# Bulk loads moved to GpSimd's queue, inputs and output laid out by partition, 19 tables packed into two transfers, first keys issued by ScalarE

## Chip, cores and metric

The kernel runs on one core of a Trainium2 chip. The metric is the device time of one execution in microseconds (us), as the median of several runs.

## What is computed

The reference is a two-layer transformer over x of shape 8 x 256 x 128, with a context of the same size and a mask of 8 x 1 x 256 x 256. Each of six sublayers is followed by a residual add and a layernorm:

```
x = LN(x + L0 self attention(x))            # 16 heads of 8, rotary angles on q and k
x = LN(x + L0 cross attention(x, ctx, ctx)) # causal, with a linear bias per head
x = LN(x + L0 ffn(x))                       # 64 of every 512 rows are picked by a router, attention + SwiGLU on them
x = LN(x + L1 self attention(x))            # with a Gaussian bias per query and head
x = LN(x + L1 cross attention(ctx, ctx, x, mask))
x = LN(x + L1 ffn(x))                       # mixture of 8 experts, top 2
```

## The kernel before, in words

Tokens lie on the 128 partitions in 16 tiles (X, f32, P x 16 x 128); XT is the same transposed. Five engines have an instruction list each, written out by hand, and are held together by semaphores.

**The first line.** The two first attention cores (`core_a0`: 8 items, `core_x0`: 8 items; one item is one batch of 256 tokens) run as one software pipeline, class `Line`, in steps; an item has 8 steps, one per pair of heads. At step s TensorE computes for item s // 8 the row maxima's scores (L616, read by VectorE's reduction L787) and, ten steps later (`LAG`), the scores again, transposed (L623 or L633), which ScalarE exponentiates (L745); TensorE then multiplies with the values (L682). The negated maxima go in as extra contraction rows: GpSimd casts them in two bf16 parts (L851, L852), TensorE turns them (L665), ScalarE copies them out (MT, L754), and SyncE (SP) writes them by DMA into the query operand (`m_rows`, L900, shown as `BIG<-MT`, two DMAs for each half item). TensorE may not start the scores of that half item before these have landed (`m_in`).

**How q and k get in.** `Split` makes three bf16 parts of each f32 projection: for each of 4 chunks of 512 tokens there are two jobs, q and k. One job is: two projections (TensorE L328), two multiplications with cos and sin (VectorE L360), their sum (GpSimd `add_turns`, L371, fbuf), first part (ScalarE L383), rest (`first_rest`, GpSimd L389, rbuf), second part (ScalarE L423), third part (GpSimd L428). SP writes the parts to DRAM (`write`, L436, rows_q and rows_k) and loads them again as operands for each item (`load`, L882: 6 DMAs for q, 6 for k, and L885: 2 of extra rows for q in the first items). Chunk 0 is done ahead of step 0, in a prologue; the others are worked in by each engine's `side(step)`.

**SP's queue.** SP works through its list in order; its `side(step)` also issues the bulk loads of what comes later: half the mask at step 6 (`Mask.load`, L1529, 1 MB), the transposed context at 13 (1 MB), the other 15 weights at 14 (0.96 MB), x at 21 (1 MB in rows of 512 bytes), the other half of the mask at 23, the context at 37, and 19 tables by one DMA each at 40, 42 and 44. TensorE, ScalarE and VectorE wait for the tables at step 63; the first use of the weights and of x is at step 39, of the transposed context at step 24 (GpSimd), of the context in `core_x0`'s values. After the last sublayer SP stores X in four DMAs (`out`, L1858).

Of the kernel before, what the change touches and what calls it, by code (L numbers as in the profile page):

```python
# [100 lines left out]
class Split:  # L101
# [283 lines left out]
    def first_rest(self, pool, n):  # L385

        pool.wait_ge(*self.s1_ready.at(n + 1))
        after(pool, self.s3_ready, n - 1)
        self.g.nc.gpsimd.tensor_tensor(self.g.rbuf[n % 2][:, :], self.source(n), self.part(n, 0), ALU.subtract)\  # L389
            .then_inc(self.r1_ready.sem, 1)  # L390
# [1123 lines left out]
class Mask:  # L1514
# [11 lines left out]
    def load(self, sp, half):  # L1526
        if half == 1:
            sp.wait_ge(*self.made.at(4))
        sp.dma_start(self.stage(half).rearrange("p (n k) -> p n k", k=S),  # L1529
                     self.g.io["mask"].rearrange("(n p) k -> p n k", p=P)[:, 8 * half:8 * half + 8, :])\  # L1530
          .then_inc(self.loaded.sem, 16)
# [107 lines left out]
class Experts:  # L1639
# [191 lines left out]
    def sync(self, sp, out):  # L1831
# [24 lines left out]
        for c in range(NC):  # L1856
            sp.wait_ge(*self.normed.at(c + 1))
            sp.dma_start(out.rearrange("(t p) d -> p t d", p=P)[:, c * TC:(c + 1) * TC, :],  # L1858
                         g.X[:, c * TC:(c + 1) * TC, :]).then_inc(self.stored.sem, 16)
# [157 lines left out]

class Globals:
# [20 lines left out]
    def allocate(self):  # L2039
# [41 lines left out]
        self.cols = sb("cols", [P, len(COLUMNS)])  # L2081
        self.rowvecs = sb("rowvecs", [P, len(ROWVECS), D])
        self.causal_q = sb("causal_q", [P, 2 * S], BF16)
        self.causal_k = sb("causal_k", [P, 2 * S], BF16)
# [6 lines left out]
        self.depth_q = sb("depth_q", [P, P], BF16)  # L2091
        self.depth_k = sb("depth_k", [P, P], BF16)
        self.router = sb("router", [P, P])
        self.earlier = sb("earlier", [P, 2, S])
        self.iota = sb("iota", [P, P])
        self.f0_w12 = sb("f0_w12", [P, 2, F0])
        self.f0_w3 = sb("f0_w3", [P, 3, D])
        self.upz = sb("upz", [P, 2 * H])
        self.router_w = sb("router_w", [P, EX])
        self.router_b = sb("router_b", [P, EX])  # L2100
        self.descending = sb("descending", [P, EX])
        self.multiples = sb("multiples", [P, T // P])
        self.up_to = sb("up_to", [P, EX, EX])
        self.upper_bf = sb("upper_bf", [P, P], BF16)
        self.ones_bf = sb("ones_bf", [P, P], BF16)
# [12 lines left out]
def program(nc, io, out):  # L2118
    with ExitStack() as ctx:
# [86 lines left out]
        def _(sp):  # L2206
# [13 lines left out]
            line.first_loads(sp, core_a0.items)  # L2220

            def side(step):
# [516 lines left out]
```

## Time and profile before

| | |
|---|---|
| median of 3 runs | 976.7 us (976.18 to 982.54) |
| profiled execution, its own time | 972.38 us |
| its span, first to last instruction | 970.5 us |
| mean granted TensorE clock | 0.871 |
| busy TensorE / VectorE / ScalarE / GpSimd | 79% / 62% / 51% / 24% of the span |
| GpSimd's DMA queue (q0), SP's (q1) | 7.21 MB, 67.18 MB |

The span is measured inside the execution, the own time around it. The busy shares are means over stages of different kinds; the first line takes the span's first 305 us or so. A "granted clock" of 1.00 is TensorE's upper level, 2.4 GHz, and 0.50 its lower, 1.2 GHz.

### The profile page before, as it was taken

Reading aid. Unit: us, or ns where it says so; the run is one execution under the profiler, and the core shown is the slowest. Engines: PE = TensorE matmul, PEld = TensorE weight load, DVE = VectorE, ACT = ScalarE, POOL = GpSimd, SP = SyncE. Lnnn points to the kernel's source line nnn. Section 1 sums busy time; section 2 is a strip of 40 time slices with the busy share of each in tenths; the row PEclk is TensorE's granted clock in tenths of the full one; section 3 lists DMA queues with packets and bytes.
Section 4 is the critical chain, followed back from the end, with each engine's and each line's share of the span. In section 5 each row is a group of like instructions: output and inputs, shape, how many; then the busy total and the mean of one; then the engine's idle time right before and its main releaser. Section 6 shows DMA issues by size and latency. Waiting matters only on the chain.

```text
span 970.5 us, 20640 instructions
## 1 busy us (share of the span) xinstructions
PE 763.2 (79%) x7108; PEld 416.7 (43%) x7109; DVE 604.1 (62%) x1908; ACT 498.5 (51%) x847; POOL 232.1 (24%) x390
## 2 busy tenths in 40 slices
PE   2687888999996645866749999999999529999950
PEld 1232323454443332434412333333334429999950
DVE  1476878667665823336348988877885344555576
ACT  1146767656556321512706877666656326665620
POOL 3344522223010120100501132323100062404223
PEclk8588999999998865956957999999999759999985
DMA  5466452242201123000532222221200611212212
GB/s 118 105 194 204 121 157 77 73 125 58 69 24 62 33 65 76 13 1 1 154 91 72 72 58 77 83 62 51 68 20 2 260 50 47 78 50 70 64 49 62
DMA packets 76075, 75.57 MB, mean 78 GB/s; under 512 B 21377, under 2 KB 65153, under 8 KB 75217
## 3 DMA queue, kind: packets, MB, share of 16 engines
q1 hardware_dynamic: 73504, 67.18, 24.1%
q0 software_dynamic: 2480, 7.21, 2.3%
q8 instruction: 54, 0.88, 0.4%
q14 instruction: 37, 0.30, 0.1%
HBM read 50.66 MB, written 23.13 MB: 76 GB/s over the span
## 4 chain that ended last, share of the span: by engine, by line
PE 61%; DVE 16%; ACT 5%; POOL 5%; issue 5%; DMA 4%; SPq 3%; POOLq 0%; DVEq 0%; ACTq 0%
PE PS L616 12%; PE PS L682 12%; PE PS L1874 8%; PE PS L633 8%; DVE MS L787 5%; PE PS L696 4%; PE PS L1884 4%; PE PS L328 2%; PE PS L623 2%; ACT X L1113 2%; POOL experts_x L1785 2%; PE PS L1047 1%; SPq L882 1%; DVE CX L804 1%; DMA OT<-experts_x 1%
## 5 line engine op out<-in xcount | busy, mean ns | idle before, releaser
L787 DVE TENSOR_REDUCE MS<-PS 128x2 f32<-128x512 f32 (+2 forms) x448 | 250.3, 592 | 130.3 <-PE PS L633 63.1
L745 ACT ACTIVATE BIG<-PS 128x1024 f32<-128x1024 f32 (+2 forms) x288 | 259.8, 906 | 63.2 <-PE PS L623 38.2
L616 PE MATMUL PS<-BIG 62*128 62x256 bf16 (+1 forms) x1088 | 199.3, 277 | 73.5 <-DMA BIG<-rows_k 16.5
L623 PE MATMUL PS<-BIG 64*128 64x256 bf16 (+1 forms) x1088 | 183.9, 269 | 1.2 <-DMA BIG<-MT 1.2
L682 PE MATMUL PS<-BIG,VA 128*32 128x256 f32 (+1 forms) x2176 | 166.7, 379 | 3.4 <-ACT OT L738 3.2
L616 PEld LDWEIGHTS PS<-BIG 62*128 62x128 bf16 x1088 | 68.5, 95 | 206.1 <-issue 97.2
L738 ACT COPY OT<-PS 128x256 f32<-128x256 f32 (+1 forms) x144 | 51.8, 360 | 117.3 <-PE PS L682 117.2
L1874 PE MATMUL PS<-OT,VA 128*128 128x128 f32 x736 | 96.7, 279 | 0.4 <-ACT OT L1931 0.4
L1874 PEld LDWEIGHTS PS<-OT,VA 128*128 128x128 f32 x736 | 91.4, 196 | 0.6 <-ACT OT L1931 0.6
L851 POOL CAST MB<-MS 128x16 bf16<-128x16 f32 (+1 forms) x72 | 14.2, 198 | 294.7 <-DVE MS L787 158.2
L682 PEld LDWEIGHTS PS<-BIG,VA 128*32 128x32 f32 x2176 | 43.4, 109 | 74.5 <-issue 63.7
L1926 ACT COPY VA<-BIG 128x1024 f32 x46 | 48.1, 1046 | 43.2 <-PE PS L1874 40.7
L623 PEld LDWEIGHTS PS<-BIG 64*128 64x128 bf16 x1088 | 64.0, 95 | 8.7 <-issue 4.0
L1965 DVE SCALAR_TENSOR_TENSOR turn<-fbuf,PS 128x512 f32<-128x512 f32 x46 | 31.6, 688 | 55.1 <-ACT fbuf L1941 55.1
L696 PE MATMUL PS<-ident,OT 128*128 128x128 f32 x272 | 59.6, 305 | 4.0 <-DVE CX L804 3.4
L782 DVE CUSTOM_DVE_ANT_0 Y<-PS,mask_q 128x256 f32<-128x256 f32 x128 | 48.8, 419 | 20.2 <-PE PS L616 19.6
L1884 PE MATMUL PS<-BIG,rbuf 128*128 x368 | 49.2, 277 | 0.9 <-DVE Y L1979 0.9
L782 DVE CUSTOM_DVE_ANT_0 HN<-PS,mask_q 128x256 f32<-128x256 f32 x128 | 48.9, 420 | 0.0
L1785 POOL DMA_INDIRECT experts_x<-X,experts_row x32 | 30.9, 965 | 72.8 <-DVE experts_row L1764 42.3
L696 PEld LDWEIGHTS PS<-ident,OT 128*128 128x128 f32 x272 | 28.0, 143 | 44.5 <-issue 41.5
L302 POOL TENSOR_TENSOR parts<-rbuf,parts 128x512 bf16<-128x512 f32 x14 | 17.1, 1224 | 124.7 <-ACT parts L227 124.6
L1884 PEld LDWEIGHTS PS<-BIG,rbuf 128*128 128x128 f32 x368 | 44.7, 192 | 1.4 <-issue 1.2
(238 smaller groups left out, 1062.6 us busy)
## 6 DMA issues: line engine op xcount, KB each, us to landing
rows_q<-parts SPq DMA_DIRECT2D x32, 192.0 KB, 2.1
rows_k<-parts SPq DMA_DIRECT2D x32, 192.0 KB, 2.1
BIG<-rows_q SPq DMA_DIRECT2D x64, 96.0 KB
BIG<-rows_k SPq DMA_DIRECT2D x64, 96.0 KB
BIG<-in_ex_w SPq DMA_DIRECT2D x3, 2048.0 KB, 12.1
BIG<-rows_q SPq DMA_DIRECT2D x64, 64.0 KB
BIG<-rows_k SPq DMA_DIRECT2D x64, 64.0 KB
OT<-experts_x SPq DMA_DIRECT2D x46, 64.0 KB, 1.8
```

The costliest lines, as they stand in the source:

```text
L616: return nc.tensor.matmul(bank[:, first:first + kw], g.Q6[b.buf][rows, u, qt * P:(qt + 1) * P], g.K6[b.buf][rows, u, 0:kw], start=start, s ...
L623: return nc.tensor.matmul(g.bank[2 * (v % 2) + a][:, core.offset[kt]:core.offset[kt] + n], g.K6[b.buf][rows, v, kt * P:(kt + 1) * P], g.Q6 ...
L633: return nc.tensor.matmul(core.biased(bank), g.ident_bf[:, :], bias, start=False, stop=True)
L682: last = nc.tensor.matmul(g.bank[6][PVW * hh:PVW * hh + PVW, lo:lo + w], g.VA[b.par][:, kt, 8 * (hh % 2) + 2 * grp + hh // 2, :], g.PT[grp ...
L696: last = nc.tensor.transpose(g.bank[7][:, grp * P:(grp + 1) * P], g.OT[b.par][:, grp, qt * P:(qt + 1) * P], g.ident[:, :])
L738: nc.scalar.copy(g.OT[b.par][:, grp, 0:w], g.bank[6][:, 0:w]).then_inc(self.ot_done.sem, 1)
L745: nc.scalar.activation(g.PT[v // 2 % 2][:, 2 * (v % 2):2 * (v % 2) + 2, 0:w], g.bank2[v % 2][:, :, 0:w], ACT.Exp, scale=SCALE).then_inc(se ...
L782: last = nc.vector.tensor_tensor_reduce(b.core.sums[a][:, 2 * qt:2 * qt + 2, :].rearrange("p n d -> p (n d)"), self.ring_bank["mx", step, ...
L787: nc.vector.tensor_reduce(g.MS[:, 0:n, a, u], self.ring_bank["mx", step, a][:, 0:n * w] .rearrange("p (n k) -> p n k", n=n), axis=AX_X, op ...
L1785: nc.gpsimd.indirect_dma_start(self.xs, bass.IndirectOffsetOnAxis(ap=self.row[:, k, n:n + 1], axis=0), g.X[:, n, :], None).then_inc(self.s ...
L1874: last = nc.tensor.matmul(g.bank[2 * a + b.par][:, f * P:(f + 1) * P], self.wb[b.par][:, a, f * P:(f + 1) * P], self.xt[b.par], start=True ...
L1884: last = nc.tensor.matmul(g.bank[6][:, 0:D], self.hid[b.par][:, f * P:(f + 1) * P], self.w3[:, bass.ds(e, 1), f, :].rearrange("p e d -> p ...
```

## The change

- The six bulk loads of the first line (both halves of the mask, transposed context, weights, x, context) are issued by GpSimd in its own `side(step)`, at the same step numbers, behind GpSimd's other work of that step.
- The mask, x and the context are stored in DRAM by partition, so that one partition's part of a transfer is one run of 8 KB; the output likewise, 2 KB in each of the four stores. The transposition is in the host's layout code.
- The 19 tables are packed into one f32 tensor (1.2 MB) and one bf16 tensor (0.39 MB), and GpSimd loads them at steps 28 and 32; the waits for them count 2 transfers in place of 19.
- In the prologue `first_rest` of the first two jobs is done by VectorE (behind its four multiplications), later ones stay on GpSimd; and the k operand of the first item is loaded from ScalarE's DMA queue, behind ScalarE's part of the prologue. SP loads that item's q and both operands of the second item.

```diff
@@ -382,11 +382,11 @@
         act.wait_ge(*self.rotated.at(n + 1))
         self.g.nc.scalar.copy(self.part(n, 0), self.source(n)).then_inc(self.s1_ready.sem, 1)
 
-    def first_rest(self, pool, n):
-
-        pool.wait_ge(*self.s1_ready.at(n + 1))
-        after(pool, self.s3_ready, n - 1)
-        self.g.nc.gpsimd.tensor_tensor(self.g.rbuf[n % 2][:, :], self.source(n), self.part(n, 0), ALU.subtract)\
+    def first_rest(self, eng, nc_eng, n):
+
+        eng.wait_ge(*self.s1_ready.at(n + 1))
+        after(eng, self.s3_ready, n - 1)
+        nc_eng.tensor_tensor(self.g.rbuf[n % 2][:, :], self.source(n), self.part(n, 0), ALU.subtract)\
             .then_inc(self.r1_ready.sem, 1)
 
     def take(self, act, n):
@@ -1526,9 +1526,7 @@
     def load(self, sp, half):
         if half == 1:
             sp.wait_ge(*self.made.at(4))
-        sp.dma_start(self.stage(half).rearrange("p (n k) -> p n k", k=S),
-                     self.g.io["mask"].rearrange("(n p) k -> p n k", p=P)[:, 8 * half:8 * half + 8, :])\
-          .then_inc(self.loaded.sem, 16)
+        sp.dma_start(self.stage(half), self.g.io["mask"][:, 8 * half * S:(8 * half + 8) * S]).then_inc(self.loaded.sem, 16)
 
     def make(self, dve, n):
 
@@ -1855,8 +1853,7 @@
         self.steps(sp, step, second_half)
         for c in range(NC):
             sp.wait_ge(*self.normed.at(c + 1))
-            sp.dma_start(out.rearrange("(t p) d -> p t d", p=P)[:, c * TC:(c + 1) * TC, :],
-                         g.X[:, c * TC:(c + 1) * TC, :]).then_inc(self.stored.sem, 16)
+            sp.dma_start(out[:, c * TC:(c + 1) * TC, :], g.X[:, c * TC:(c + 1) * TC, :]).then_inc(self.stored.sem, 16)
         sp.wait_ge(*self.stored.at(16 * NC))
...
@@ -2013,6 +2010,20 @@
            "x1_q", "x1_k", "x1_v", "x1_o", "f0_q", "f0_k", "f0_v", "f0_o"]
 COLUMNS = ["a1_bq", "a1_bk", "a1_bfq", "a1_bfg", "f0_g1", "f0_g2"]
 ROWVECS = ["a1_bv", "a1_bo", "x1_bo"]
+
+
+TABLES = {
+    F32: [("cols", (len(COLUMNS),)), ("router", (P,)), ("iota", (P,)), ("upz", (2 * H,)), ("router_w", (EX,)),
+          ("router_b", (EX,)), ("descending", (EX,)), ("multiples", (T // P,)), ("rowvecs", (len(ROWVECS), D)),
+          ("up_to", (EX, EX)), ("earlier", (2, S)), ("f0_w12", (2, F0)), ("f0_w3", (3, D))],
+    BF16: [("causal_q", (2 * S,)), ("causal_k", (2 * S,)), ("depth_q", (P,)), ("depth_k", (P,)),
+           ("upper_bf", (P,)), ("ones_bf", (P,))],
+}
+
+
+def tables_width(dt):
+
+    return sum(int(np.prod(shape)) for _, shape in TABLES[dt])
 
 
...
-        self.f0_w3 = sb("f0_w3", [P, 3, D])
-        self.upz = sb("upz", [P, 2 * H])
-        self.router_w = sb("router_w", [P, EX])
-        self.router_b = sb("router_b", [P, EX])
-        self.descending = sb("descending", [P, EX])
-        self.multiples = sb("multiples", [P, T // P])
-        self.up_to = sb("up_to", [P, EX, EX])
-        self.upper_bf = sb("upper_bf", [P, P], BF16)
-        self.ones_bf = sb("ones_bf", [P, P], BF16)
+        self.tables = {dt: sb(f"tables_{n}", [P, tables_width(dt)], dt) for n, dt in enumerate(TABLES)}
+        place = {}
+        for dt, entries in TABLES.items():
+            first = 0
+            for name, shape in entries:
+                w = int(np.prod(shape))
+                ap = self.tables[dt][:, first:first + w]
+                place[name] = ap if len(shape) == 1 else ap.rearrange("p (a b) -> p a b", a=shape[0])
+                first += w
+        self.cols, self.router, self.iota, self.upz = (place[n] for n in ("cols", "router", "iota", "upz"))
+        self.router_w, self.router_b = place["router_w"], place["router_b"]
+        self.descending, self.multiples = place["descending"], place["multiples"]
+        self.rowvecs, self.up_to, self.earlier = place["rowvecs"], place["up_to"], place["earlier"]
+        self.f0_w12, self.f0_w3 = place["f0_w12"], place["f0_w3"]
+        self.causal_q, self.causal_k = place["causal_q"], place["causal_k"]
+        self.depth_q, self.depth_k = place["depth_q"], place["depth_k"]
+        self.upper_bf, self.ones_bf = place["upper_bf"], place["ones_bf"]
 
...
@@ -2217,7 +2226,8 @@
             sp.dma_start(g.ident[:, :], io["ident"]).then_inc(ident_in.sem, 16)
             for n in range(2):
                 split_a0.write(sp, n)
-            line.first_loads(sp, core_a0.items)
+            line.load(sp, core_a0.items[0], "q")
+            line.load(sp, core_a0.items[1])
 
...
                             split_a0.write(sp, 2 * c + i)
-                if step == 6:
-                    mask.load(sp, 0)
-                if step == 13:
-                    sp.dma_start(g.CTXT[:, :], io["ctxt"]).then_inc(ctxt_in.sem, 16)
-                if step == 14:
-                    sp.dma_start(g.W[:, n_a0:, :], io["weights"][:, n_a0:, :]).then_inc(weights_in.sem, 16)
-                if step == 21:
-                    sp.dma_start(g.X[:, :, :], io["x"].rearrange("(t p) d -> p t d", p=P)).then_inc(x_in.sem, 16)
-                if step == 23:
-                    mask.load(sp, 1)
-                if step == 37:
-                    sp.wait_ge(*mask.made.at(8))
-                    sp.dma_start(g.CTX[:, :, :], io["ctx"].rearrange("(t p) d -> p t d", p=P)).then_inc(ctx_in.sem, 16)
-                if step == 40:
-                    for ap, name in ((g.cols, "cols"), (g.causal_q, "causal_q"), (g.causal_k, "causal_k"),
-                                     (g.depth_q, "depth_q"), (g.depth_k, "depth_k"), (g.router, "router"), (g.iota, "iota")):
-                        sp.dma_start(ap[:, :], io[name]).then_inc(tables_in.sem, 16)
-                if step == 42:
-                    for ap, name in ((g.upz, "upz"), (g.router_w, "router_w"), (g.router_b, "router_b"),
-                                     (g.descending, "descending"), (g.multiples, "multiples"), (g.upper_bf, "upper_bf"),
-                                     (g.ones_bf, "ones_bf")):
-                        sp.dma_start(ap[:, :], io[name]).then_inc(tables_in.sem, 16)
-                if step == 44:
-                    for ap, name in ((g.rowvecs, "rowvecs"), (g.up_to, "up_to"), (g.earlier, "earlier"), (g.f0_w12, "f0_w12"),
-                                     (g.f0_w3, "f0_w3")):
...
-                    pe.wait_ge(*tables_in.at(16 * 19))
+                    pe.wait_ge(*tables_in.at(16 * 2))
                 post_x0.run("tensor", pe, step)
...
+            line.load(act, core_a0.items[0], "k")
 
             def side(step):
...
+            split_a0.first_rest(dve, nc.vector, 0)
+            split_a0.first_rest(dve, nc.vector, 1)
 
             def side(step):
...
-            split_a0.first_rest(pool, 0)
             split_a0.third_part(pool, 0)
-            split_a0.first_rest(pool, 1)
             split_a0.third_part(pool, 1)
 
...
+                if step == 6:
+                    mask.load(pool, 0)
+                if step == 13:
+                    pool.dma_start(g.CTXT[:, :], io["ctxt"]).then_inc(ctxt_in.sem, 16)
+                if step == 14:
+                    pool.dma_start(g.W[:, n_a0:, :], io["weights"][:, n_a0:, :]).then_inc(weights_in.sem, 16)
+                if step == 21:
+                    pool.dma_start(g.X[:, :, :], io["x"]).then_inc(x_in.sem, 16)
+                if step == 23:
+                    mask.load(pool, 1)
+                if step == 37:
+                    pool.wait_ge(*mask.made.at(8))
+                    pool.dma_start(g.CTX[:, :, :], io["ctx"]).then_inc(ctx_in.sem, 16)
+                if step in (28, 32):
+                    n = step // 4 - 7
+                    pool.dma_start(g.tables[F32 if n == 0 else BF16][:, :], io[f"tables_{n}"]).then_inc(tables_in.sem, 16)
...
-    io["mask"] = a["mask_Bx1xSxS2_if1"].reshape(B * S, S)
-    io["x"] = a["x"].reshape(T, D)[:, DFIRST]
-    io["xt"] = io["x"].T
-    io["ctx"] = a["ctx_1024"].reshape(T, D)[:, DFIRST]
-    io["ctxt"] = io["ctx"].T
+    by_partition = lambda rows: rows.reshape(-1, P, rows.shape[1]).transpose(1, 0, 2)
+    io["mask"] = by_partition(a["mask_Bx1xSxS2_if1"].reshape(B * S, S)).reshape(P, -1)
+    x = a["x"].reshape(T, D)[:, DFIRST]
+    io["x"], io["xt"] = by_partition(x), x.T
+    ctx = a["ctx_1024"].reshape(T, D)[:, DFIRST]
+    io["ctx"], io["ctxt"] = by_partition(ctx), ctx.T
     return io
...
 
-    arrays = {n: np.ascontiguousarray(v) for n, v in
-              (layout({k: np.asarray(v) for k, v in inputs.items()}) | constants()).items()}
+    arrays = layout({k: np.asarray(v) for k, v in inputs.items()}) | constants()
+    for n, (dt, entries) in enumerate(TABLES.items()):
+        arrays[f"tables_{n}"] = np.concatenate([np.asarray(arrays.pop(name)).reshape(P, -1).astype(mybir.dt.np(dt))
+                                                for name, _ in entries], axis=1)
+    arrays = {n: np.ascontiguousarray(v) for n, v in arrays.items()}
     nc = _bacc.Bacc("TRN2", target_bir_lowering=False, num_devices=1)
     io = {n: nc.dram_tensor(f"in_{n}", v.shape, mybir.dt.from_np(v.dtype), kind="ExternalInput").ap()
           for n, v in arrays.items()}
-    out = nc.dram_tensor("out_0", (T, D), F32, kind="ExternalOutput").ap()
+    out = nc.dram_tensor("out_0", (P, NT, D), F32, kind="ExternalOutput").ap()
     program(nc, io, out)
     r = _run(nc, [{f"in_{n}": v for n, v in arrays.items()}], core_ids=[0])
-    return r.results[0]["out_0"][:, np.argsort(DFIRST)].reshape(B, S, D)
+    rows = np.asarray(r.results[0]["out_0"]).transpose(1, 0, 2).reshape(T, D)
```

## Rows read from the trace of the kernel before

**Rows 1.** The page: busy time of each engine, share of the span, instructions.

```profile
PE 763.2 (79%) x7108; PEld 416.7 (43%) x7109; DVE 604.1 (62%) x1908; ACT 498.5 (51%) x847; POOL 232.1 (24%) x390
```

**Rows 2.** TensorE's waits, 80 to 100 us: waited for, total, times, longest.

```profile
PE PS L616 <- DMA BIG<-MT: 4.4, 1, 4.4
```

**Rows 3.** TensorE's waits, 140 to 160 us.

```profile
PE PS L616 <- DMA BIG<-MT: 3.1, 1, 3.1
```

**Rows 4.** Windows of 2 us: busy per engine, then clock, DMA share, GB/s.

```profile
92.00:94.00 2.00, 0.47 (x4) 0.13 (x4) 0.00 (x0) 0.00 (x0) 0.00 (x0) 0.50 1.10 358
94.00:96.00 2.00, 2.00 (x18) 0.50 (x18) 0.97 (x2) 0.61 (x2) 0.00 (x0) 0.50 0.85 197
96.00:98.00 2.00, 2.00 (x17) 0.40 (x16) 1.11 (x2) 1.02 (x2) 0.00 (x0) 0.50 0.20 57
...
142.00:144.00 2.00, 2.00 (x22) 0.60 (x22) 1.19 (x2) 0.83 (x2) 0.00 (x0) 0.72 0.51 117
144.00:146.00 2.00, 2.00 (x17) 0.53 (x14) 0.98 (x3) 0.86 (x3) 0.00 (x0) 0.50 0.04 8
```

**Rows 5.** Timeline of the prologue: start, us, instruction, idle before it.

```profile
13.00 1.26 POOL L371 TENSOR_TENSOR fbuf<-CX 128x512 f32<-128x512 f32 x1 [0.56 <-DVE CX L360]
14.29 0.62 ACT L383 CAST parts<-fbuf 128x512 bf16<-128x512 f32 x1 [1.21 <-POOL fbuf L371]
...
15.93 0.58 ACT L344 COPY V<-PS 128x512 f32<-128x512 f32 x1
...
19.09 1.15 POOL L428 TENSOR_TENSOR parts<-rbuf,parts 128x512 bf16<-128x512 f32 x1 [0.73 <-ACT parts L423]
...
24.41 2.20 SPq L882 DMA_DIRECT2D BIG<-rows_k  x6
...
29.62 0.61 PE L616 MATMUL PS<-BIG 62*128 62x256 bf16 x4 [16.54 <-DMA BIG<-rows_k]
```

**Rows 6.** The DMA view: issues, count, KB each, median us to landing.

```profile
rows_k<-parts SPq DMA_DIRECT2D x32, 192.0 KB, 2.1
...
out<-X SPq DMA_DIRECT2D x4, 256.0 KB, 2.3
...
X<-in_x SPq DMA_DIRECT2D x1, 0.5 KB, 6.5
```

**Rows 7.** SP's queue, 83 to 89 and 121 to 140 us.

```profile
83.17 2.27 SPq L882 DMA_DIRECT2D BIG<-rows_q  x6
85.79 0.87 SPq L2237 DMA_DIRECT2D X<-in_x  x1
86.70 2.10 SPq L900 DMA_DIRECT2D BIG<-MT  x2
...
121.30 0.40 SPq L2246 DMA_DIRECT2D cols<-in_cols  x1
...
136.75 2.17 SPq L882 DMA_DIRECT2D BIG<-rows_q  x6
138.96 1.27 SPq L900 DMA_DIRECT2D BIG<-MT  x2
```

**Rows 8.** ScalarE's copies of the maxima (MT) ahead of the two stalls.

```profile
85.33 0.34 ACT L754 COPY MT<-PS 16x256 bf16<-16x256 bf16 x1
...
135.13 0.34 ACT L754 COPY MT<-PS 16x256 bf16<-16x256 bf16 x1
```

**Rows 9.** GpSimd's timeline at the shortest and a later gap.

```profile
71.43 1.15 POOL L389 TENSOR_TENSOR rbuf<-fbuf,parts 128x512 f32<-128x512 f32 x1 [0.97 <-ACT parts L383]
...
86.70 0.20 POOL L851 CAST MB<-MS 128x16 bf16<-128x16 f32 x1 [3.31 <-DVE MS L787]
```

**Rows 10.** 1 MB issued by GpSimd (line 1714), and SP's queue just behind it.

```profile
L1714 POOL DMA_DIRECT2D experts_x<-CTX x3: 531/665/819, 193.6 to 289.5; - x3
...
194.95 2.68 SPq L882 DMA_DIRECT2D BIG<-rows_q  x3
```

**Rows 11.** Window of 15 us in the early part of the line.

```profile
45.00:60.00 15.00, 12.96 (x46) 3.74 (x45) 10.33 (x17) 2.71 (x5) 6.29 (x8) 0.70 0.62 183
```

More of the change, by code:

```diff
@@ L2080, in allocate @@
         self.W = sb("W", [P, len(WEIGHTS), P])
[L2081 to L2084, printed above, removed]
         PS = self.ctx.enter_context(nc.psum_tensor("PS", [P, 8, CH], F32))
@@ L2090, in allocate @@
         self.mask_k = sb("mask_k", [P, B * 2 * S], BF16)
[L2091 to L2096, printed above, removed]
-        self.f0_w3 = sb("f0_w3", [P, 3, D])
-        self.upz = sb("upz", [P, 2 * H])
-        self.router_w = sb("router_w", [P, EX])
-        self.router_b = sb("router_b", [P, EX])
-        self.descending = sb("descending", [P, EX])
-        self.multiples = sb("multiples", [P, T // P])
-        self.up_to = sb("up_to", [P, EX, EX])
-        self.upper_bf = sb("upper_bf", [P, P], BF16)
-        self.ones_bf = sb("ones_bf", [P, P], BF16)
+        self.tables = {dt: sb(f"tables_{n}", [P, tables_width(dt)], dt) for n, dt in enumerate(TABLES)}
[15 more added lines that the diff above has]
+        self.upper_bf, self.ones_bf = place["upper_bf"], place["ones_bf"]
     def w(self, name):
@@ L2229, in side @@
                             split_a0.write(sp, 2 * c + i)
-                if step == 6:
-                    mask.load(sp, 0)
-                if step == 13:
-                    sp.dma_start(g.CTXT[:, :], io["ctxt"]).then_inc(ctxt_in.sem, 16)
-                if step == 14:
-                    sp.dma_start(g.W[:, n_a0:, :], io["weights"][:, n_a0:, :]).then_inc(weights_in.sem, 16)
-                if step == 21:
-                    sp.dma_start(g.X[:, :, :], io["x"].rearrange("(t p) d -> p t d", p=P)).then_inc(x_in.sem, 16)
-                if step == 23:
-                    mask.load(sp, 1)
-                if step == 37:
-                    sp.wait_ge(*mask.made.at(8))
-                    sp.dma_start(g.CTX[:, :, :], io["ctx"].rearrange("(t p) d -> p t d", p=P)).then_inc(ctx_in.sem, 16)
-                if step == 40:
-                    for ap, name in ((g.cols, "cols"), (g.causal_q, "causal_q"), (g.causal_k, "causal_k"),
-                                     (g.depth_q, "depth_q"), (g.depth_k, "depth_k"), (g.router, "router"), (g.iota, "iota")):
-                        sp.dma_start(ap[:, :], io[name]).then_inc(tables_in.sem, 16)
-                if step == 42:
-                    for ap, name in ((g.upz, "upz"), (g.router_w, "router_w"), (g.router_b, "router_b"),
-                                     (g.descending, "descending"), (g.multiples, "multiples"), (g.upper_bf, "upper_bf"),
-                                     (g.ones_bf, "ones_bf")):
-                        sp.dma_start(ap[:, :], io[name]).then_inc(tables_in.sem, 16)
-                if step == 44:
-                    for ap, name in ((g.rowvecs, "rowvecs"), (g.up_to, "up_to"), (g.earlier, "earlier"), (g.f0_w12, "f0_w12"),
-                                     (g.f0_w3, "f0_w3")):
-                        sp.dma_start(ap[:, :, :], io[name]).then_inc(tables_in.sem, 16)
                 for c in range(NC):
@@ L2431, in side @@
                 if step == 63:
-                    act.wait_ge(*tables_in.at(16 * 19))
+                    act.wait_ge(*tables_in.at(16 * 2))
                 post_x0.run("scalar", act, step)
@@ L2491, in side @@
                 if step == 63:
-                    dve.wait_ge(*tables_in.at(16 * 19))
+                    dve.wait_ge(*tables_in.at(16 * 2))
                 post_x0.run("vector", dve, step)
@@ L2554, in side @@
                     if at == 1:
-                        split_a0.first_rest(pool, 2 * c)
+                        split_a0.first_rest(pool, nc.gpsimd, 2 * c)
                     if at == 2:
@@ L2560, in side @@
                     if at == 4:
-                        split_a0.first_rest(pool, 2 * c + 1)
+                        split_a0.first_rest(pool, nc.gpsimd, 2 * c + 1)
                     if at == 5:
@@ L2734 @@
           for n, v in arrays.items()}
-    out = nc.dram_tensor("out_0", (T, D), F32, kind="ExternalOutput").ap()
+    out = nc.dram_tensor("out_0", (P, NT, D), F32, kind="ExternalOutput").ap()
     program(nc, io, out)
     r = _run(nc, [{f"in_{n}": v for n, v in arrays.items()}], core_ids=[0])
-    return r.results[0]["out_0"][:, np.argsort(DFIRST)].reshape(B, S, D)
+    rows = np.asarray(r.results[0]["out_0"]).transpose(1, 0, 2).reshape(T, D)
+    return rows[:, np.argsort(DFIRST)].reshape(B, S, D)
```

## The prediction, made before the change was run

> **What bounds the kernel now.** The page first: TensorE is busy for 763 of 970 us, 79% [rows 1]; but that is a mean over stages, and the change touches only the first line and its prologue, so I read those. TensorE's waits between 80 and 200 us name, apart from short ones, one releaser twice: `BIG<-MT`, the small transfer that brings the maxima's rows into the queries, 4.4 us before about 93.5 [rows 2] and 3.1 us before about 142.0 [rows 3]. Both times the other engines run dry too, and the windows of 2 us show what follows: the granted clock is 0.50, TensorE's lower level (1.2 GHz), from 92 to 98, after nearly 4 us without a matmul, and again around 144 [rows 4]. TensorE is busy in all of the windows 94:96 and 96:98 at that clock, VectorE and ScalarE in half: half of the time is lost. Stall 1 thus costs 4.4 + (0.47 + 4)/2 = 6.6 us. In stall 2 the window 142:144 has 0.72, so 1.1 of its 2 us are at the lower level, 144:146 all 2: 3.1 + 3.1/2 = 4.7 us.
>
> Why the rows are late is read in SP's queue. **Stall 1:** MT is in SBUF at 85.67 (85.33 + 0.34) [rows 8], but SP is at the load of x then, and issues MT from 86.70, in 2.10 us in place of the 1.27 that it takes later [rows 7]. In its queue it stands behind x, 1 MB in pieces of 0.5 KB, 6.5 us to landing [rows 6]: 85.79 + 6.5 = 92.3, and MT lands a little later. **Stall 2:** MT is there at 135.47 [rows 8]. SP has been issuing 19 tables since 121.30, then issues a load of rows_q from 136.75, and MT from 138.96, 3.5 us late [rows 7].
>
> The prologue is a chain of another kind: no operand, no first score before 29.62 [rows 5].
>
> **The change part by part.**
>
> *Prologue.* Now the sum of the second job is done at 14.26, ScalarE's first part at 14.91, and both rests and both third parts are taken by GpSimd in turn, until 20.24 (19.09 + 1.15) [rows 5]. With the rests on VectorE, which has nothing else to do then, even at GpSimd's 1.15 us each [rows 9] the first is done before 14.95 and the second by 16.1. ScalarE then has second part (0.62), values (0.58), second part (0.62) in a row: 14.95 to 16.85. GpSimd's last third part runs 16.9 to 18.05: 2.2 us earlier. The second saving is in the issues. Before, SP issued the first item's q and then, from 24.41, its k, done at 26.61, and the first score began 3.0 us later [rows 5]. Now k waits for its own write alone: second write issued at 18.6, 2.1 us to landing [rows 6], 20.7; six issues at SP's rate (2.20) end at 22.9. q on SP: its write lands at about 19.5, eight issues at that rate are 2.9 us, 22.4. So the last issue comes at 22.9 in place of 26.6, 3.7 us earlier. No row shows ScalarE issuing a DMA: at SP's 0.37 each the gain is 3.7; at the 0.82 that GpSimd takes at most [rows 10] six take 4.9 and the gain is 1.0. SP is the nearest in kind; I take 3.5. ScalarE has nothing to do meanwhile: its next copy follows TensorE's first projection in the line. SP comes to the second item and the last two pieces of XT some 3.6 us earlier, none of which is waited for now.
>
> *X and half the mask off SP (stall 1).* SP is free at 85.44 and issues MT at 85.7, as soon as it is there. Issues of 1.3 and a landing like that of other small transfers, 2.1 [rows 6], give 89.1, and TensorE wanted it at 93.5 - 4.4 = 89.1. But x and the mask, 2 MB, start on GpSimd's queue at about 84 and 85, and at the 358 GB/s of the window 92:94 [rows 4] they run until about 91. What MT meets then is the open term. Ends: nothing (6.6 gained) and the whole stall, as if queued behind x (0 gained). Nearest row: with 1 MB issued by GpSimd at 193.6, SP's next three issues took 2.68 us [rows 10], in place of 1.1: the bulk holds SP's queue back by 1.6 us, without stopping it. I take a stall of 1.6 us left, no fall of the clock: 5.0 gained. The Trainium skill, page "DMA: Bandwidth & Descriptors", section "Issuing engines are not separate DMA queues", speaks against this term: transfers of all issuing engines run on the same 16 DMA engines, and another issuer saves only the issue time. By it the 1.0 us of issue (86.70 - 85.7) would be gained of the 6.6, and the sum would be 9.2. The same page, section "Queues, rings and completion order", says that an engine takes turns between its queues packet by packet, which is my side.
>
> *Tables off SP (stall 2).* The 19 issues go, the rows_q load comes at once, and MT is issued at 135.5, lands near 138.9, when it is wanted (142.0 - 3.1). The tables now go at steps 28 and 32, near 100 and 106, when no MT was late. Gained: 3.1 at least if the clock falls anyway, 4.7 at most; I take 4.5.
>
> *GpSimd's new work.* Eight DMAs; the one kind that the trace has, 1 MB with 8 KB in a partition, holds GpSimd for 0.53 to 0.82 us [rows 10]. Their places: behind step 6 (a long gap follows), steps 13 and 14 around 67 and 70.5, where the shortest gap is 0.97 before 71.43, still over 0.82; steps 21 and 23, where 3.31 us are idle before 86.70 [rows 9]; 28, 32 and 37 ahead of GpSimd's waits for VectorE. Cost nothing; if a gap were missed, 0.8 us once. At step 37 GpSimd waits for the mask's eighth piece, as SP did; behind it are two pieces of the fourth key job, not written until step 41. The wait for four pieces at step 23 is over long before.
>
> *Longer runs in DRAM.* Same bytes, fewer pieces: it shortens x and context off the path. The last store (256 KB, 2.3 us to landing [rows 6]) is on the path at the very end; 0 to 1 us, I take 0.2. Fewer waits on table counts: nothing.
>
> **Sum:** 3.5 + 5.0 + 4.5 + 0.2 = 13.2 us, against the profiled execution's own 972.4 (span 970.5): 959.2. The median of the runs shown is 976.7, 4.3 above that execution; from it 963.5, which I forecast. All stages behind, from about 190 us, are as before.
>
> **Rivals.**
>
> - *The bulk still holds MT* (same engines): MT comes 1.0 us earlier, by its earlier issue alone. 3.5 + 1.0 + 4.5 + 0.2 = 9.2 gained, 967.5. This is the first rule of the page above. For it: the DMA engines are full at 92 to 94 [rows 4], whoever issues. Against: in the trace MT was behind x in one queue, and no longer is. Chance 0.2.
> - *The clock.* From 45 to 60 it is 0.70 on average [rows 11], so it changes level there; begun 3.5 us earlier it may fall otherwise. If all 15 us were at 0.50, the 10.5 us of full-speed work would take 21: 6 lost, 7.2 gained, 969.5. Nothing speaks for it over its opposite. 0.1.
> - *All clear*: MT lands in time and the issues are as quick as SP's: 3.7 + 6.6 + 4.7 + 1 = 16.0, 960.7. 0.12.
> - *Slower: row loads and MT caught beside the bulk on GpSimd's queue.* The mask near 48, context and weights at 67 to 72, x and mask at 84, tables at 100 and 106, context at 116: each can stretch SP's issues by the 1.6 us above and more, and wherever MT lands over 3.4 us after its copy TensorE stops and the clock falls. Each such place costs the mean of the two, 5.6. Against the 9.2 just worked out, two new ones make it 2.0 us slower (978.7), and four (989.9) slower by over 1%. Against it: before, the transposed context stood ahead of an MT in SP's own queue, and TensorE's waits name no stall from it. 0.07.
> - *The prologue's or the tables' part does not come* (ScalarE's issues slow, or stall 2 only moved elsewhere): 5 to 9 gained, 968 to 972. 0.08.
>
> **How the numbers follow.** The forecast has the remaining 0.43. About 1%, 9.8 us, is what a measurement of this kernel can tell from no change. Faster by more: forecast and all clear, and a little of the others' edge, 0.57. Slower by over 1%: 0.07 and nothing else. Within 1%: 0.36. The range takes in all clear from the lower level of the profiled execution (956) and the third and fourth kind of rival up to 973: 955 to 973.
>
> **What would show it.** First L616 at 26 us; VectorE's subtractions at 13 to 16 us; no wait of TensorE for BIG<-MT over 2 us and no window at 0.50 between 60 and 190; MT issued within 0.3 us of ScalarE's copy in SP's queue; GpSimd's DMA rows at 0.5 to 0.8 us. Wrong if: a wait for BIG<-MT, rows_k or MB (through GpSimd) appears at one of the bulk's new places, the first score still comes at 28 or later, or stages behind 300 us change length.

## The result: half a per cent at most, where 13.2 us were forecast

The changed kernel took 974.0 us (median of 12 runs, 970.95 to 977.23), the kernel before 978.66 us in the same series (12 runs); the ratio is 0.9949, 95% interval 0.9927 to 0.9971. In a second series it was 977.1 against 978.52, ratio 0.9970 (0.9935 to 1.0006). So the changed kernel is faster by 4.7 and 1.4 us between the medians, or 5.0 and 2.9 us by the ratios, and the second interval takes in no change at all. That is within the 1% that was called no change, and not the 13.2 us that the sum gave; 974.0 also lies above the range.

The profiled execution has a span of 975.4 us and an own time of 977.23, the longest of its 12; the one shown of the kernel before, 972.4, lies below all 12 of this series. So the spans can't be set against each other. The page of the changed kernel (busy time, share, instructions) has TensorE 3.3 us busier than [rows 1] for the same matmuls, though 22 of its records are missing. More time at the lower clock would do that; the mean granted clock was 0.860 in place of 0.871:

```profile
PE 766.5 (79%) x7086; PEld 419.3 (43%) x7109; DVE 603.6 (62%) x1910; ACT 497.5 (51%) x847; POOL 232.5 (24%) x396
```

Both stalls' places have changed: one wait has grown, one is gone, and a new one has come. TensorE's waits of the changed kernel (waited for, total, times, longest), 80 to 100 us:

```profile
PE PS L616 <- DMA BIG<-MT: 6.8, 1, 6.8
```

and of the same kernel, 100 to 120 us:

```profile
PE PS L616 <- DMA BIG<-MT: 2.3, 1, 2.3
```

The wait of 2.3 us, near 112, is new. Between 140 and 160 us no transfer is left among the waits, where 3.1 us stood [rows 3]. But the wait of 4.4 us [rows 2] has grown to 6.8. The windows of 2 us behind it, columns as in [rows 4]:

```profile
90.00:92.00 2.00, 0.07 (x1) 0.00 (x0) 0.97 (x3) 0.80 (x1) 1.76 (x2) 1.00 1.11 281
92.00:94.00 2.00, 0.00 (x0) 0.00 (x0) 0.00 (x0) 0.00 (x0) 0.00 (x0) 0.50 0.94 227
94.00:96.00 2.00, 0.00 (x0) 0.00 (x0) 0.00 (x0) 0.00 (x0) 0.00 (x0) 0.50 0.70 178
96.00:98.00 2.00, 1.17 (x12) 0.33 (x12) 0.53 (x1) 0.00 (x0) 0.00 (x0) 0.50 0.13 41
98.00:100.00 2.00, 2.00 (x21) 0.57 (x18) 0.98 (x3) 1.32 (x3) 0.00 (x0) 0.50 0.00 0
100.00:102.00 2.00, 2.00 (x16) 0.48 (x10) 1.14 (x2) 0.86 (x3) 0.00 (x0) 0.50 0.01 2
```

TensorE stands still for some 7 us and then runs at the lower level (0.50, 1.2 GHz) to 102, against 98 before [rows 4]. By the prediction's own way of counting (the wait, and half of TensorE's busy time at the lower level behind it), stall 1 costs 6.8 + (1.17 + 2 + 2)/2 = 9.4 us in place of 6.6. The second profile of the changed kernel (e11 below) gives 8.3 by the same count, and the two repeated profiles of the kernel before give 6.8 and 6.9. MT is late again, but for another reason. The timeline of the changed kernel (start, us, instruction), GpSimd:

```profile
84.02 0.55 POOL L2568 DMA_DIRECT2D X<-in_x  x1
84.56 0.54 POOL L1529 DMA_DIRECT2D CTX<-in_mask  x1
```

ScalarE, the copy that makes MT:

```profile
86.28 0.34 ACT L754 COPY MT<-PS 16x256 bf16<-16x256 bf16 x1
```

and SP's queue:

```profile
84.12 2.54 SPq L882 DMA_DIRECT2D BIG<-rows_q  x6
86.70 1.29 SPq L900 DMA_DIRECT2D BIG<-MT  x2
```

The chain of waits of the changed kernel (start, us, what) has two landings of MT:

```profile
87.37 9.41 DMA BIG<-MT
...
109.02 4.99 DMA BIG<-MT
```

and that of the kernel before had, at the same place:

```profile
88.19 5.29 DMA BIG<-MT
```

SP now issues MT 0.1 us after ScalarE's copy has ended (86.62), in 1.29 us, as wanted. It takes 9.41 us to land in place of 5.29. These two count from the end of MT's first issue, which was itself held for 1.45 us before and 0.63 now; from the end of ScalarE's copy to the landing it is 10.2 us in place of 7.8 (85.67 to 93.48). The difference to before: SP had x ahead of MT and the mask's second half behind it (issued at 88.85); GpSimd comes to these steps more than 2 us before SP and issues both ahead of MT, at 84.0 and 84.6.

To set executions side by side, two marks serve, since stages behind the first line take different times from one execution to the next (the last section): the first score (first L616) and the end of the first line (first L1200, 317.90 in the kernel before, 319.36 in the changed). Between them lie 288.3 us before and 289.2 after. The first score itself came at 30.16 us, where 26 was forecast and 29.62 had been: the eight projections in front of it ended at 14.13 in place of 12.19. They are the same in every kernel and took 5.3 to 6.7 us in the fourteen profiles, so the prologue is counted from their end.

### The profile page after: what moved, and what is told of

It reads as the page before. It is cut to its first block, busy times and chain, and to the rows that moved or that the text cites. A ratio compares the mean times of both kernels' runs of the same rounds, so it can differ in the third digit from the quotient of the medians.

```text
span 975.4 us, 20599 instructions
## 1 busy us (share of the span) xinstructions
PE 766.5 (79%) x7086; PEld 419.3 (43%) x7109; DVE 603.6 (62%) x1910; ACT 497.5 (51%) x847; POOL 232.5 (24%) x396
## 4 chain that ended last, share of the span: by engine, by line
PE 62%; DVE 15%; ACT 5%; POOL 5%; DMA 5%; issue 5%; SPq 2%; ACTq 0%; POOLq 0%; DVEq 0%
PE PS L682 12%; PE PS L616 12%; PE PS L1871 8%; PE PS L633 8%; DVE MS L787 4%; PE PS L1881 4%; PE PS L696 4%; PE PS L328 2%; PE PS L623 2%; ACT X L1113 2%; DMA BIG<-MT 2%; POOL experts_x L1783 1%; ACT BIG L745 1%; PE PS L1047 1%; DVE CX L804 1%
## 5 line engine op out<-in xcount | busy, mean ns | idle before, releaser
L616 PE MATMUL PS<-BIG 62*128 62x256 bf16 (+1 forms) x1088 | 200.1, 279 | 72.6 <-DMA BIG<-rows_k 15.1
L616 PEld LDWEIGHTS PS<-BIG 62*128 62x128 bf16 x1088 | 68.5, 96 | 206.8 <-issue 98.1
L633 PE MATMUL PS<-tables,ident_bf 128*128 128x256 bf16 (+1 forms) x384 | 59.7, 276 | 0.0
```

The lines of the kernel that those rows point to most:

```text
L616: return nc.tensor.matmul(bank[:, first:first + kw], g.Q6[b.buf][rows, u, qt * P:(qt + 1) * P], g.K6[b.buf][rows, u, 0:kw], start=start, s ...
L633: return nc.tensor.matmul(core.biased(bank), g.ident_bf[:, :], bias, start=False, stop=True)
```

## The experiments

Each measured ratio is to the kernel before. "To the first score" is from the end of the eight projections (L328) of the prologue, in us; "waits for MT" are TensorE's, between 60 and 200 us; "the line" is from the first score to the first L1200. The last three columns are read from one profile of each run, and from three and two of the first two rows.

| kernel | ratio (95%) | to the first score | waits for MT | the line |
|---|---|---|---|---|
| before, three profiles | 1 | 17.4, 17.9, 17.9 | 4.4+3.1, 4.1+4.1, 4.5+4.9 | 288.3, 289.2, 292.5 |
| changed, two profiles | 0.9949, 0.9970 | 16.0, 16.0 | 6.8+2.3, 6.5 | 289.2, 287.1 |
| e1_prologue | 0.9987 (0.9964 to 1.0009) | 16.8 | 3.8+4.2 | 290.1 |
| e2_bulk | 0.9925 (0.9900 to 0.9950) | 17.8 | 6.9, 0.3 | 288.6 |
| e3_gated | 0.9899 (0.9857 to 0.9942) | 16.2 | 2.3 | 283.7 |
| e4_layout_sp | 0.9892 (0.9865 to 0.9919) | 17.9 | 2.3 | 282.6 |
| e5_sp_both | 0.9904 (0.9867 to 0.9942) | 17.9 | 5.9 | 285.3 |
| e6_mask27 | 0.9884 (0.9840 to 0.9928) | 16.3 | 2.8 | 283.9 |
| e7_behind_mt | 0.9827 (0.9796 to 0.9858) | 15.2 | none | 281.4 |
| e9_k_alone | 0.9836 (0.9784 to 0.9887) | 15.5 | 0.6, 0.2 | 281.4 |
| e10_tables | 0.9907 (0.9876 to 0.9938) | 17.8 | 3.6 | 283.9 |

### First four: which part brings what

**e1_prologue.** The kernel before, and of the change:

```diff
+            split_a0.first_rest(dve, nc.vector, 0)
+            split_a0.first_rest(dve, nc.vector, 1)
+            line.load(act, core_a0.items[0], "k")
-            line.first_loads(sp, core_a0.items)
+            line.load(sp, core_a0.items[0], "q")
+            line.load(sp, core_a0.items[1])
```

> The kernel before with the prologue's part of the change alone: VectorE takes the first two rests, ScalarE issues the first item's k. Theory A (as predicted, the two shorten the chain to the first score by about 3 us): time 3 us below before, ratio 0.997. Theory B (k on a second queue shares the 16 DMA engines with the second item's loads that SP now issues at once, so k lands about 5 us after its last issue instead of 3, and the gain is used up): ratio 0.999 to 1.001, first score at 28 to 30 us.

Measured 0.9987, which can't be told from nothing. 16.8 us to the first score against 17.4 to 17.9: it comes about 1 us earlier and not 3, which is the case of theory B. The last issue of k is at 23.42 and the first score at 29.41, 6.0 us later, where it was 3.0 before. The timeline of e1_prologue, ScalarE's issues of k, SP's of the second item, the first score:

```profile
20.90 2.52 ACTq L882 DMA_DIRECT2D BIG<-rows_k  x6
...
24.33 1.11 SPq L882 DMA_DIRECT2D BIG<-rows_q  x3
...
29.41 0.61 PE L616 MATMUL PS<-BIG 62*128 62x256 bf16 x4 [15.89 <-DMA BIG<-rows_k]
```

**e2_bulk.** The changed kernel without those lines.

> The changed kernel with the prologue as before; bulk loads on GpSimd's queue, layouts and packed tables stay. Theory B of the prologue: the whole measured gain of 5 us stays here, ratio 0.995. Theory A: only about 1.5 us stay, ratio 0.998. In the profile, both: one wait for BIG<-MT of 6 to 7 us near 96 us, none near 142.

0.9925: the gain stays without the prologue's part. The wait is 6.9 us, as expected. But the parts don't add up: e1 and e2 together would make 0.991, and the changed kernel, which is both, has 0.9949 and 0.9970; its medians (974.0, 977.1) lie above e2's 971.6. The last section comes back to this.

**e3_gated.** The changed kernel; GpSimd waits for an MT's landing ahead of each bulk load but the first:

```diff
+                if step in (12, 16, 20, 24, 28, 32, 40):
+                    k, half = divmod(step - 8, 8)
+                    ...
+                    pool.wait_ge(*line.m_in[b.buf][half].at((b.use + 1) * 32))
-                if step == 23:
+                if step == 24:
                     mask.load(pool, 1)
```

> The changed kernel with each bulk load on GpSimd's queue but the first held until a BIG<-MT transfer has landed (steps 12, 16, 20, 24, 28, 32, 40 in place of 13, 14, 21, 23, 28, 32, 37), so at most one bulk load of about 1 MB is under way between two BIG<-MT transfers, and x and the second half of the mask are no longer both ahead of one. Theory C (a small transfer lands only when the bulk issued before it, in whichever queue, is nearly through): no wait for BIG<-MT over 1.5 us between 60 and 190 us, no window at the lower clock there, 6 to 10 us faster than the changed kernel, ratio to before 0.985 to 0.989. Rival D (bulk on GpSimd's queue holds SP's transfers back by itself, at any place and order): waits of 3 us and more move to other places, ratio 0.994 to 1.0.

The wait falls from 6.8 to 2.3 us and the one near 112 is gone; the line is 3.4 to 5.5 us shorter than in the changed kernel's two profiles. 0.9899, not quite the 0.985 to 0.989 of theory C, and a wait of 2.3 us where it allowed 1.5: x alone still stands ahead of the MT of step 22.

**e4_layout_sp.** Layouts and packed tables, all on SP's queue at the old steps, tables at 40 and 42, the old prologue.

> The kernel before with the layouts by partition and the packed tables only: all bulk loads and the two table transfers stay on SP's queue at the old steps (tables at 40 and 42), prologue as before. Theory C: the wait near 93 stays (x still ahead of BIG<-MT, 3 to 5 us), the one near 142 is 0 to 3 us since 1.2 MB are issued ahead of a BIG<-MT there; ratio 0.994 to 0.998, no worse than with GpSimd's queue. Rival D: without GpSimd's queue the wait near 93 is shorter than the 6.8 us of the changed kernel by 2 us or more and the kernel is faster than the changed one, ratio below 0.992. If neither queue nor order matters but only the issue time on SP: ratio 0.998 to 1.0.

0.9892, better than the changed kernel by about 6 us, with one wait of 2.3 us. Theory C had forecast 0.994 to 0.998 and missed; this looked like rival D. But on SP's queue the order was also the old one, x, MT, mask. The next two separate them.

### Order or queue

**e5_sp_both.** e4 with the mask issued right behind x, on SP's queue:

```diff
                 if step == 21:
                     sp.dma_start(g.X[:, :, :], io["x"]).then_inc(x_in.sem, 16)
+                    mask.load(sp, 1)
-                if step == 23:
-                    mask.load(sp, 1)
```

> The kernel of e4_layout_sp (everything on SP's queue) with one edit: the second half of the mask is issued at step 21 right behind x, so 2 MB stand ahead of the BIG<-MT transfer of step 22, as GpSimd issued them in the changed kernel. Theory C (what is issued ahead, in whichever queue, delays it): the wait for BIG<-MT near 95 grows from 2.3 to 5.5 to 7.5 us, time 4 to 7 us above e4. Rival D (GpSimd's queue does the harm): the wait stays at 2 to 3.5 us, time as e4.

TensorE's waits of e5_sp_both, 80 to 100 us:

```profile
PE PS L616 <- DMA BIG<-MT: 5.9, 1, 5.9
```

SP's queue of e5_sp_both, x, mask, MT:

```profile
86.93 0.36 SPq L2246 DMA_DIRECT2D X<-in_x  x1
87.34 0.43 SPq L1529 DMA_DIRECT2D CTX<-in_mask  x1
87.81 1.29 SPq L900 DMA_DIRECT2D BIG<-MT  x2
```

and its chain of waits:

```profile
88.48 7.96 DMA BIG<-MT
```

5.9 us: the long stall comes back without GpSimd's queue. The time, 970.1, is 2.7 us over e4's, under the 4 to 7 forecast, and the intervals overlap. So the return of the stall is shown by the profile, and not by the time.

**e6_mask27.** The changed kernel, mask's second half at step 27 in place of 23, on GpSimd's queue.

> The changed kernel with one edit: GpSimd issues the second half of the mask at step 27 in place of 23, so x alone is ahead of the BIG<-MT transfer of step 22. Theory C: the wait near 96 falls from 6.8 to 1.5 to 3.5 us; a new one of up to 3 us may come behind the mask, at step 30 or so. Rival D: it stays over 5 us, since GpSimd's queue holds SP's back with 1 MB as well.

TensorE's waits of e6_mask27, 80 to 100 us:

```profile
PE PS L616 <- DMA BIG<-MT: 2.8, 1, 2.8
```

GpSimd's issues in e6_mask27, x and then the mask:

```profile
82.97 0.56 POOL L2568 DMA_DIRECT2D X<-in_x  x1
...
90.74 0.55 POOL L1529 DMA_DIRECT2D CTX<-in_mask  x1
```

and its chain of waits:

```profile
86.28 5.52 DMA BIG<-MT
```

2.8 us, and the ratio falls to 0.9884, by changing the number of one step. Rival D falls: with 1 MB ahead MT lands in 4.45 to 5.52 us on either queue (e4 4.87, e10 4.45, e3 4.96, e6 5.52; before 5.29), with 2 MB ahead in 7.96 (SP) and 8.90 to 9.61 (GpSimd: changed kernel twice, e2). These count from the end of MT's first issue. From the end of ScalarE's copy it is 5.8 us (e4, SP's queue) and 5.7 and 6.2 (e3 and e6, GpSimd's) with 1 MB ahead in runs of 8 KB, and 9.3 (e5, SP's) and 9.9 to 10.3 (GpSimd's) with 2 MB. So with the same bytes ahead the queue made no difference at 1 MB, and GpSimd's queue may add some 1 us at 2 MB; that stays open.

**e7_behind_mt.** The version that this points to: e4, with VectorE's two rests, k on SP, and each bulk load moved right behind the next MT:

```diff
-                if step == 21:
+                if step == 22:
                     sp.dma_start(g.X[:, :, :], io["x"]).then_inc(x_in.sem, 16)
-                if step == 23:
+                if step == 26:
                     mask.load(sp, 1)
```

(context transposed 13 to 14, weights 14 to 18, context 37 to 38, tables at 30 and 42.)

> A version after theory C: layouts and packed tables, all bulk on SP's queue, each issued right behind a BIG<-MT transfer (steps 6, 14, 18, 22, 26, 38, tables at 30 and 42), VectorE takes the first two rests, the first item's k stays on SP's queue. Theory C: no wait for BIG<-MT over 1 us between 60 and 190 us, first score 2 us earlier than in e4 at the same clock; ratio to before 0.980 to 0.986, faster than e4. Rival D: the same as e4, 0.988 to 0.991, but for the prologue's 2 us. If a third thing bounds the line (the writes or row loads behind the bulk in the same queue): a wait for BIG<-rows_k or rows_q appears and the ratio is over 0.99.

0.9827 (0.9796 to 0.9858), 962.86 us: 17 us faster than the kernel before in its series, and clear of the changed kernel's interval. TensorE's waits in e7_behind_mt between 60 and 200 us, the seven largest:

```profile
PE PS L616 <- DVE MS L787: 3.7, 9, 1.4
PE PS L1128 <- ACT X L1113: 1.3, 2, 0.6
PE PS L616 <- ACT V L344: 1.2, 2, 0.9
PE PS L682 <- ACT OT L738: 1.1, 2, 0.5
PE PS L616 <- ACT BIG L745: 0.9, 1, 0.9
PE PS L665 <- ACT mask_k L1553: 0.7, 2, 0.4
PE PS L616 <- DVE CX L360: 0.5, 1, 0.5
```

No transfer is among these, nor among the smaller ones. Several things changed at once here: against e4 the first score comes 2.7 us sooner and the line is 1.2 us shorter, 3.9 us of the 6 us or so between the two ratios.

### Controls, and the prologue

**e8_before_again, e12_before_third and e11_after_again**: both kernels unchanged.

> The kernel before, unchanged, for a second profile and as a control of the timing: ratio 0.997 to 1.003. Its first line (to the first matmul of line 1200) ended at 317.9 us in the profile shown, which was faster than nearly all its other executions. If the scatter lies in the first line's stalls it ends at 320 to 325 here; if it lies in the stages behind, it ends at 317 to 319 and those take 655 us or more in place of 652.6.

> The kernel before, unchanged, for a third profile: the waits for BIG<-MT at 4.1 to 4.4 us near 93 and 3 to 4.2 us near 142 come again; first line ends at 318 to 321 us.

> The changed kernel, unchanged, for a second profile. If the waits near 96 and 112 are the rule and not chance of the first profile, they come again at 6 to 7.5 us and 2 to 7 us. The stage from the last line of line one to rows_x took 35.1 us in its first profile and 29.6 in most others; at 29.6 the span is about 970.

The kernel before against itself: 1.0003 (0.9966 to 1.0039) and 0.9981 (0.9944 to 1.0019). Its two waits come each time, the second at 3.1, 4.1 and 4.9 us; with the time at the lower level behind it stall 2 costs 4.7, 5.8 and 7.5 us, so it was dearer than the profile shown had it. In e8 the line ended at 319.95 us and the stages behind took 658 in place of 652.6: part of the scatter lies in each. In e12 the line came out longer than any other (ended at 323.74, where 318 to 321 were expected), with that second wait of 4.9. The changed kernel's first wait comes again (6.5), the second does not.

**e10_tables.** The kernel before with the two packed table transfers alone, on SP's queue at steps 40 and 42.

> The kernel before with the packed tables alone, on SP's queue at steps 40 and 42; inputs and output laid out as before. Theory C with the layouts as a cause of their own: the wait near 142 is gone, the one near 93 stays at 4 to 4.5 us (2.3 in e4_layout_sp, where x's runs are 8 KB), ratio 0.993 to 0.996. If the layouts do nothing: the wait near 93 falls to 2.3 here too, ratio as e4, 0.989.

0.9907. The wait near 142 is gone, the one near 93 stays at 3.6: between the two readings, so by one profile each the longer runs of x account for about 1.3 us of a wait (3.6 to 2.3 in e4), and the tables for most of e4's gain. The ratio is better than the forecast 0.993 to 0.996. What shorter runs cost is seen in SP's queue, issues of x and then MT. In e10_tables, x in runs of 0.5 KB:

```profile
86.26 0.87 SPq L2249 DMA_DIRECT2D X<-in_x  x1
87.17 2.23 SPq L900 DMA_DIRECT2D BIG<-MT  x2
```

and in e4_layout_sp, in runs of 8 KB:

```profile
89.16 0.36 SPq L2246 DMA_DIRECT2D X<-in_x  x1
89.57 1.29 SPq L900 DMA_DIRECT2D BIG<-MT  x2
```

**e9_k_alone.** e7 with k on ScalarE's queue, and SP waiting for the whole first item:

```diff
-            line.first_loads(sp, core_a0.items)
+            line.load(sp, core_a0.items[0], "q")
+            sp.wait_ge(*line.feat[0].at(core_a0.items[0].feat))
+            line.load(sp, core_a0.items[1])
```

> The kernel of e7_behind_mt with the first item's k on ScalarE's queue again, and SP's loads of the second item held until the whole first item has landed. The measure is the time from the end of the eight projections to the first score: 17.4 to 17.9 us in five executions with the old prologue, 16.0 to 16.8 in four with the changed one, 15.2 in e7. Theory B (on a second queue k shares the DMA engines with the second item's loads): without these it lands 3 us after its last issue, 13.5 to 14.5 us from projections to score, ratio 0.5 to 1.5 us better than e7, 0.981. Rival (a ScalarE issue is slow to land by itself): 15.8 to 16.8 us again, ratio 0.984.

15.5 us, between the two, and no better than e7's 15.2. ScalarE's last issue of k ends at 24.93, the first score is at 29.24, 4.3 us later; in e7, from SP's queue, 24.81 and 27.67, 2.9 us; in the changed kernel, e1, e3 and e6, with the second item's loads beside it, 4.8 to 6.0. So the second item's loads may explain the part above 4.3 us, and a slower landing from ScalarE's queue the part above 2.9; by single profiles, and no run here takes the two apart further.

## Why the prediction failed, step by step

**What it had right.** The two stalls, and for stall 2 its cause in SP's queue (the tables' packing alone gives 0.9907, and the wait near 142 is gone with it); that the issue of MT would follow the copy at once; GpSimd's work hidden, at 0.54 to 0.73 us an issue. The rests at VectorE: 17.4 to 17.9 us became 15.2 in e7, 2.2 to 2.7 gained where 2.2 were forecast.

**Stall 1 is the step that failed**, 5.0 us forecast as gain; by the profiles it costs more than before (9.4 and 8.3 us against 6.6 to 6.9). The prediction noted that both x and the mask would start near 84 and 85, and then priced what MT meets by a row with 1 MB behind it [rows 10], as a stretch of SP's issues: 1.6 us of stall left. TensorE waited 6.8 and 6.5 us. The step asked how the bulk holds SP's issues back and not how long an issued transfer takes to land. The rows had the case with 1 MB ahead: MT issued from 86.70 [rows 7] and the score waiting for it at 93.5 [rows 2, 4]; its landing alone took 5.29 us. With 2 MB ahead it is 8 to 9.6. Nor were the 2 MB through at about 91, as 358 GB/s gave: in the windows above the transfers go on until about 97, at 178 to 281 GB/s from 90 to 96, and MT lands as they end (96.78). The six loads of rows_q, from 84.12, share that time too. What mattered was not the queue but the order: on SP the mask came behind MT, on GpSimd, which is a step or more ahead, it came in front. e5 (SP, both ahead, 5.9 us) and e6 (GpSimd, one ahead, 2.8 us) show this in both directions.

The prediction had set two sections of the page "DMA: Bandwidth & Descriptors" of the Trainium skill against each other. The measurement decides for the section "Issuing engines are not separate DMA queues": another issuer saved at most the 1.0 us of issue, and with x in runs of 8 KB not even that, for SP then issued MT 0.2 us after the copy by itself (e4). The turns between queues of "Queues, rings and completion order" gave MT no lead that any run shows. That section also says that a transfer's semaphore increment lands only after every earlier write of its DMA engine, across queues; the 9.4 us agree with that, and with mere sharing of the engines as well. No run here separates the two.

The rival "the bulk still holds MT" (0.2) was the right kind, but was priced at 967.5 with stall 1 otherwise unchanged. The stall grew: what the forecast lacked on top of it was the order.

**Stall 2**: 4.5 us forecast. The wait is gone in both profiles of the changed kernel, but the first has another, 2.3 us near 112, behind the first of the packed tables (1.2 MB), which GpSimd issues at 103.2, 5.2 us ahead of MT's issue. With the lower clock behind it (0.50 and 0.68 in the windows from 116 to 120, TensorE busy throughout) it costs some 3.9 us and takes back most of the term. This would be the slower rival's mechanism, once: in the second profile, with the same order, TensorE doesn't wait there. The term itself was sized rightly or low, from e10's line of 283.9 against 288.3 to 292.5.

**Prologue**: 3.5 us forecast, 1.4 to 1.9 measured (16.0 against 17.4 to 17.9). The rests gave 2.2 to 2.7. The k operand on ScalarE's queue gave back 0.8 to 1.6 (e7's 15.2 against 16.0 to 16.8) where 1.3 were forecast as gain: the last issue was earlier, the landing was not. The prediction took the 3.0 us from last issue to score as fixed; it was 2.9 with k issued from SP's queue ahead of the second item's loads, and 4.8 to 6.0 with k on ScalarE's queue and the second item's loads beside it.

**Behind the line.** The prediction left all stages behind about 190 us as before, and named a change of length there as a sign of being wrong. In both profiles of the changed kernel one of them was 5 us longer, at a lower granted clock (the last section). Whether the change does that is not shown.

**Sum.** Prologue 1.7 and a line shorter by 290.0 (mean of 288.3, 289.2, 292.5) - 288.2 (mean of 289.2, 287.1) = 1.8 make 3.5 us, by single profiles that differ by 2 to 4 among themselves; the two series give 4.7 and 1.4 us between the medians. The last store's 0.2 us can't be seen.

## What to carry to other kernels

A transfer moved to a faster-running queue also moves in time: list what small, awaited transfers are issued behind it in all queues together, and price each by the bytes ahead, from a row where it lands behind as many. Here, changing the queue saved at most the issue time, while placing each bulk load directly behind the awaited transfer left none of those waits. And the load that was split over two queues wasn't finished as much sooner as its last issue, since what used to follow it now ran beside it.

## What the runs showed that was not expected

VectorE and GpSimd held each other up in the new prologue. In e1_prologue VectorE's two subtractions from SBUF, beside GpSimd's sum of 1.26 us (start, us, instruction):

```profile
13.44 1.26 POOL L371 TENSOR_TENSOR fbuf<-CX 128x512 f32<-128x512 f32 x1 [0.56 <-DVE CX L360]
13.56 2.52 DVE L389 TENSOR_TENSOR rbuf<-fbuf,parts 128x512 f32<-128x512 f32 x2 [0.20 <-ACT parts L383]
```

and in the changed kernel, where VectorE began first, GpSimd's sum took 1.64:

```profile
14.78 0.68 DVE L389 TENSOR_TENSOR rbuf<-fbuf,parts 128x512 f32<-128x512 f32 x1
14.94 1.64 POOL L371 TENSOR_TENSOR fbuf<-CX 128x512 f32<-128x512 f32 x1 [1.55 <-DVE CX L360]
```

Alone they take 0.69 (VectorE's second subtraction in the changed kernel, at 17.26) and 1.26. The Trainium skill, page "SBUF — State Buffer", section "SBUF: two separate sides", has this as a lock: a VectorE operation with two SBUF inputs and a GpSimd operation that reads SBUF don't run together. By that rule, the trace agrees: whichever began second was longer. In e1 it cost the chain nothing, since ScalarE was busy until it took up the second rest at 16.28. In the changed kernel ScalarE was waiting for that sum, so its 0.38 us count in full.

Stages whose code the change doesn't touch took one of a few lengths. Ahead of the second layer, from SP's write of rows_f to that of rows_q, it was 103.9 to 105.6 us, once 109.5 (e8). In the second layer, from that first write of rows_q to that of rows_x, it was 29.6 to 30.0 us in ten profiles and 34.9 to 35.1 in four: the changed kernel's two, e3 and e9. The granted clock goes with this. Two windows of the kernel before, 12 to 28 us after the first write of rows_q (462.00):

```profile
474.00:482.00 8.00, 6.68 (x34) 4.27 (x34) 2.04 (x5) 5.41 (x12) 7.57 (x7) 1.00 0.60 169
482.00:490.00 8.00, 2.71 (x24) 2.48 (x24) 4.15 (x13) 1.23 (x4) 0.68 (x1) 0.64 0.76 222
```

and of the changed kernel, at the same distance from its write (465.80):

```profile
477.80:485.80 8.00, 6.38 (x17) 3.52 (x18) 2.00 (x5) 3.96 (x9) 7.07 (x7) 0.71 0.69 164
485.80:493.80 8.00, 6.84 (x27) 5.67 (x25) 0.40 (x2) 2.33 (x6) 0.59 (x1) 0.50 0.80 228
```

In all four long ones the clock falls to the lower level within 16 us of that write, in the ten others only after 20 us or more, and TensorE then takes longer for the same matmuls (eight of L1440 1.55 us in place of 0.81). What makes it fall earlier is not shown. All four are among the six profiles in which ScalarE's queue issues the first k; none of the eight without it has it. That may be chance, no run tests it, and it may be why the changed kernel is slower than e2, which is the same but for the prologue. Single profiles therefore can't be compared by their spans; that is why this document compares marks.
